# A dynamic 1x1 convolution on one Trainium2 core: the hidden layer's sum over partitions moved off TensorE

## What is computed

```
B, C, H, W = 32, 512, 56, 56;  A = 32 hidden units;  K = 4 kernels
g = group_norm(x, 32 groups)                         # x: (B, 512, 56, 56) float32
pooled = mean(g, over H, W)
h = relu(((pooled @ fc_w.T) - abn_m) * abn_g / sqrt(abn_v + eps) + abn_b)    # first attention layer
ch_att, fl_att = sigmoid(h @ ch_w.T + ch_b), sigmoid(h @ fl_w.T + fl_b)
kn_att = softmax(h @ kn_w.T + kn_b)
agg_w = sum_k kn_att[k] * weight[k]                  # one 512 x 512 matrix for each sample
y = (agg_w @ (g * ch_att)) * fl_att                  # 1x1 convolution
out = x + batch_norm(y)
```

## Time and profile before

| | |
|---|---|
| median of 3 runs | 2103.95 us (2103.34 to 2104.27) |
| span of the profiled execution | 2101.4 us |
| the same, with what lies around the span (the runs' median less the span) | 2.5 us more |
| PE busy | 2054.3 us (98%), 10848 matmuls |
| DVE busy | 1898.9 us (90%) |
| ACT busy | 1726.0 us (82%) |
| POOL busy | 12.8 us (1%) |
| DMA, mean busy share and rate | 58.3% of 16 engines in SyncE's queue, 198 GB/s of HBM traffic |
| mean granted TensorE clock | 0.996 |

### The profile page before, as it was taken

How to read it: one execution, slowest core, us unless ns; L and a number is a source line. 1 busy time by engine, 2 the same in 40 slices (tenths; PEclk the granted TensorE clock), 3 DMA queues, 4 the chain that set the end, 5 groups by cost and what they waited for, 6 DMA issues and landing times.

```text
span 2101.4 us, 33109 instructions
## 1 busy us (share of the span) xinstructions
PE 2054.3 (98%) x10848; PEld 1061.1 (50%) x10848; DVE 1898.9 (90%) x3065; ACT 1726.0 (82%) x2307; POOL 12.8 (1%) x25
## 2 busy tenths in 40 slices
PE   3979999999999999999999999999999999999999
PEld 2535555555555555555555555555555555555554
DVE  8879999999999999999999999999999999999974
ACT  5858888888888888888888888888888888888885
POOL 0100000000000000000000000000000000000000
PEclk9999999999999999999999999999999999999999
DMA  9976656565556565556655566655565655566522
GB/s 334 224 217 207 207 189 206 204 210 199 195 199 206 196 210 196 205 193 209 208 195 203 188 205 207 210 196 194 200 206 199 210 194 204 195 208 207 180 105 106
DMA packets 239644, 421.60 MB, mean 201 GB/s; under 512 B 7552, under 2 KB 236928, under 8 KB 239616
## 3 DMA queue, kind: packets, MB, share of 16 engines
q1 hardware_dynamic: 237888, 415.74, 58.3%
q0 software_dynamic: 1728, 5.51, 1.4%
HBM read 210.19 MB, written 205.52 MB: 198 GB/s over the span
## 4 chain that ended last, share of the span: by engine, by line
PE 93%; DMA 5%; DVE 1%; ACT 1%; SPq 0%; issue 0%; POOL 0%; DVEq 0%; POOLq 0%
PE product L854 31%; PE product L856 31%; PE product L855 31%; DMA out<-x_ring 3%; DMA x_ring<-x 1%; DMA x_ring<-y 1%; PE small L821 0%; SPq L216 0%; DVE chunk_stats L441 0%; ACT w_hi L344 0%; ACT x_norm L262 0%; DVE mixed_weight L625 0%; ACT x_hi L328 0%; DVE x_ring L455 0%; ACT x_hi L271 0%
## 5 line engine op out<-in xcount | busy, mean ns | idle before, releaser
L854 PE MATMUL product<-x_hi,w_hi 128*128 128x448 f16 x3552 | 1253.2, 353 | 11.7 <-DVE x_lo L449 10.3
L855 PE MATMUL product<-x_lo,w_hi 128*128 128x448 f16 x3552 | 1253.1, 353 | 0.0
L856 PE MATMUL product<-x_hi,w_lo 128*128 128x448 f16 x3552 | 1253.0, 353 | 0.0
L283 ACT ACTIVATE y<-product,out_bias,out_scale 128x448 f32<-128x448 f32 x892 | 638.7, 716 | 262.3 <-PE product L856 259.0
L262 ACT ACTIVATE x_norm<-x_ring,norm_bias,norm_scale 128x448 f32<-128x448 f32 x892 | 668.2, 750 | 0.0
L455 DVE TENSOR_TENSOR x_ring<-x_ring,y 128x896 f32<-128x896 f32 x434 | 465.4, 1084 | 80.3 <-ACT y L283 76.0
L854 PEld LDWEIGHTS product<-x_hi,w_hi 128*128 128x128 f16 x3552 | 350.3, 99 | 337.8 <-DVE x_lo L449 11.2
L441 DVE BATCH_NORM_STATS2 chunk_stats<-x_ring 128x6 f32<-128x448 f32 x896 | 492.2, 612 | 22.6 <-DMA x_ring<-x 20.4
L856 PEld LDWEIGHTS product<-x_hi,w_lo 128*128 128x128 f16 x3552 | 347.8, 98 | 324.1 <-issue 1.3
L855 PEld LDWEIGHTS product<-x_lo,w_hi 128*128 128x128 f16 x3552 | 347.8, 98 | 321.1 <-issue 2.9
L449 DVE TENSOR_TENSOR x_lo<-x_norm,x_hi 128x1792 f16<-128x1792 f32 x222 | 447.6, 2016 | 14.9 <-ACT x_hi L271 14.9
(11 more groups left out here) (93 smaller groups left out, 327.8 us busy)
## 6 DMA issues: line engine op xcount, KB each, us to landing
x_ring<-x SPq DMA_DIRECT2D x224, 896.0 KB, 4.8
out<-x_ring SPq DMA_DIRECT2D x223, 896.0 KB, 3.9
x_ring<-y POOLq DMA_DIRECT2D x12, 448.0 KB, 7.5
weight<-wt SPq DMA_DIRECT2D x8, 512.0 KB, 12.9
out<-x_ring SPq DMA_DIRECT2D x4, 224.0 KB, 1.9
params<-par SPq DMA_DIRECT2D x1, 462.0 KB, 12.1
```

The costliest lines, as they stand in the source:

```text
L283: nc.scalar.activation(y[:, s % 2, t], acc[k % BANKS][:, 0:COLS], ACT.Identity, bias=obias[:, t:t + 1], scale=oscale[:, u, t:t + 1]).then_ ...
L854: nc.tensor.matmul(bank, whi[:, u, t, cols], hi, start=(t == 0), stop=False)
L855: nc.tensor.matmul(bank, whi[:, u, t, cols], lo, start=False, stop=False)
L856: ins = nc.tensor.matmul(bank, wlo[:, u, t, cols], hi, start=False, stop=(t == CT - 1))
```

## The change

From the third sample on, the first layer's sum over partitions is made in another way. VectorE turns `fc_sums` in blocks of 32 x 32 (`fcs_t`), so that partition 32q + a holds hidden unit a's 32 terms of quarter q, and sums them to one number for each partition (`fcq`). SyncE writes these 128 numbers to HBM (`rows`), waits until they have landed, and reads them back, all 128 into each partition (`hidq`). VectorE sums the four quarters. For this SyncE has a new step between the load at n = 2 and the store of chunk n = 3, and the steps from `logits` on have later places in `usual`. The first two samples keep the matmul.

More of the change, by code:

```diff
@@ L140, in build @@
         hid_p = small[:, 256:256 + HIDDEN]
+        rows = nc.dram_tensor("hidden_rows", (P,), f32).ap()
         top_row, top_all = small[0:1, 64:64 + P], small[:, 200:201]
@@ L170, in build @@
         pooled_ready = sem("pooled_ready")
+        rows_order = sem("rows_order")
+        hid_summed = sem("hid_summed")
+        fcq_ready = sem("fcq_ready")
+        rows_out = sem("rows_out")
+        rows_in = sem("rows_in")
         logits_ready = sem("logits_ready")
@@ L512, in group_var, with norms @@
                 step(nc.vector.tensor_copy(gm[:, :], grouped[:, 0, 0:CT, 0]))
-            def norms(turn, b):
+            def norms(turn, b, on_pe):
                 u = b % 2
@@ L526, in norms, with logits @@
                 after(turn)
-                nc.vector.tensor_reduce(fcs[:, :], fcp[:, :, :].rearrange("p t a -> p a t"), AX.X,
-                                        ALU.add).then_inc(pooled_ready, 1)
-            def logits(turn, b):
-                dve.wait_ge(hid_done, turn.at(2, b + 1))
-                step(nc.vector.tensor_tensor(hid[:, :], hid_p, p_("abn_m"), ALU.subtract))
+                ins = nc.vector.tensor_reduce(fcs[:, :], fcp[:, :, :].rearrange("p t a -> p a t"), AX.X, ALU.add)
+                if on_pe:
+                    ins.then_inc(pooled_ready, 1)
+                    return
+                ins.then_inc(rows_order, 1)
+                dve.wait_ge(rows_order, turn.at(4, 2 * b - 3))
+                nc.vector.transpose(fcs_t[:, :], fcs[:, :]).then_inc(rows_order, 1)
+                dve.wait_ge(rows_order, turn.at(4, 2 * b - 2))
+                nc.vector.reduce_sum(fcq[:, :], fcs_t[:, :], AX.X).then_inc(fcq_ready, 1)
+            def logits(turn, b, on_pe):
+                if on_pe:
+                    dve.wait_ge(hid_done, b + 1)
+                    step(nc.vector.tensor_tensor(hid[:, :], hid_p, p_("abn_m"), ALU.subtract))
+                else:
+                    dve.wait_ge(rows_in, turn.at(32, 16 * (b - 1)))
[3 more added lines that the diff above has]
+                    step(nc.vector.tensor_tensor(hid[:, :], hid[:, :], p_("abn_m"), ALU.subtract))
                 after(turn)
@@ L609, in _ @@
             group_var(start, 0)
-            norms(start, 0)
+            norms(start, 0, True)
             dve.wait_ge(bn_ready, 1)
-            logits(start, 0)
+            logits(start, 0, True)
             attentions(start, 0)
@@ L731, in body @@
                         if prepare and (n, t) == at["norms"]:
-                            norms(turn, b)
+                            norms(turn, b, at is early)
                         if prepare and (n, t) == at["att"]:
@@ L749, in body @@
                             if (n, t) == at["logits"]:
-                                logits(turn, b)
+                                logits(turn, b, at is early)
                             if (n, t) in at["mix"]:
@@ L817, in _, with hidden @@
         def _(pe):
-            def hidden(turn, b):
-                pe.wait_ge(pooled_ready, turn.at(2, b + 1))
+            def hidden(b):
+                pe.wait_ge(pooled_ready, b + 1)
                 nc.tensor.matmul(hid_p, ones[:, :], fcs[:, :], start=True, stop=True).then_inc(hid_done, 1)
@@ L825, in _ @@
             pe.wait_ge(const_ready, 1)
-            hidden(start, 0)
+            hidden(0)
             def keep_awake(n):
```

4 lines of the change are left out of this document (added).

## The result

The changed kernel takes 2314.77 us (median of 4 runs, 2314.19 to 2318.12), against 2103.66 for the kernel before on the same chip: a ratio of 1.101 (95% interval 1.0997 to 1.1024), 211 us slower. Predicted were 2147 us and a range up to 2172. The sign was right, the size was not: the forecast of +43 was a fifth of what happened, and the prediction is wrong.

A forecast was written before the change was run, and what follows sets the result against it. TensorE was taken to bound the kernel. Per sample -0.25 + 0.18 + 1.51 = +1.44 us, times 30 = +43.2, gave 2147 us, with the transfers costing nothing; the range given was 2136 to 2172.

The forecast's parts named there:

- What goes: On TensorE, the matmul of ones leaves 30 samples, saving 0.25 us each, 7.5 us in all.
- VectorE ahead of chunk 4: VectorE's turning and sum delay chunk 4's x_lo by 0.46 us, making TensorE wait 0.18 us per sample.
- The new places: Chain from ScalarE's mix to chunk 7's x_lo ends later; TensorE waits 1.51 us in each of 30 samples.
- the term of the loss: TensorE's wait for x_lo of chunk 7, each sample's first chunk: 1.51 us, the largest term of +1.44 per sample.
- The two transfers: SyncE's write and read behind the load: rows there at 991.8, in time for VectorE, costing nothing.
- its upper end of 996.6: Latest landing of the read, taking full chunks' landings of 3.9 and 4.8 us behind the load.
- The text's second estimate: Rows' arrival at 992.0 instead of 991.8, from a cited fixed cost of about 2.0 us per transfer; still in time.
- The one-for-one rule: Each microsecond the rows land past 992.2 delays attentions, mix and all behind by one; one late microsecond gives 2177.
- Rival 2: Rows land late at VectorE: up to 4.4 us a sample, +132, a time of 2279; chance 0.10.
- 992.2: Latest time the transfers may land without delaying VectorE's logits and the attentions, on the profiled sample's clock.
- the room of 0.2: Attentions are there at 996.5, 0.2 us before ScalarE's mix can start, so the rows have that slack.
- Rival 4: TensorE's clock falls at each new wait: 3.2 us each, +95 more, a time of 2242; chance 0.02.

The follow-up runs named there:

- experiment 1: Kernel before with only the later places of the changed one, matmul of ones kept, no transfers: 2151.73 us against 2102.21.
- experiment 2: Changed kernel with both transfers left out, the quarter sums VectorE adds being a constant: 2150.05 us, ratio 1.0226.
- experiment 4: Changed kernel with each of the 128 numbers written to, and each partition reading, a 512-byte HBM line of its own: 2149.81 us.
- experiment 5: Changed kernel with VectorE turning the sums once more, so they leave as 4 rows of 128 bytes: 2158.05 us against 2102.95.
- experiment 7: Changed kernel writing the 128 numbers into one SBUF partition and reading an HBM row never rewritten: 2152.04 us (one run).
- experiment 11: Changed kernel with 34 idle matmuls ahead of chunk 6's first product in the 14 middle turns: 2351.71 us, ratio 1.1194.
- experiment 3: Changed kernel with the write issued ahead of the load of chunk n = 2 instead of behind it: 2311.33 us, ratio 1.0998.
- experiment 9: Changed kernel writing only the first 64 of the 128 four-byte pieces, the rest a constant: 2300.95 us (one run).
- experiment 12: Changed kernel with four 128-byte rows, w_hi and w_lo at (6, 0) and (6, 1), turnings behind chunk 4's x_lo: 2132.95 us against 2102.02.

## Why the prediction was wrong

**What goes: right.** 30 matmuls of 0.25 us. Experiments 1 and 2 show the exchange: with the matmul a sample loses 1.60 us, without it 1.60 + 0.22 - 0.25, and the two times differ by 1.7 us, less than their spread.

**VectorE ahead of chunk 4: right.** Laid out were 0.18 us, measured 0.22. The turning and the sum stand at 0.41 and 0.66 behind `fc_sums`' start (1010.38, 1010.79, 1011.04), as laid out.

**The new places: right.** 1.51 laid out, 1.60 measured, in experiments 1, 2 and 4. The step that I had named as the term of the loss is there, when the rows are in time.

**The two transfers: the step that failed.** "I take the shortest landing twice, but behind the load in the same queue: 987.9 + 1.9 + 0.1 + 1.9 = 991.8." The rows came 12.9 us after the quarter sums ended (1011.23 to 1024.13), in the text's own clock at 997.0 instead of 991.8, and 0.4 past its upper end of 996.6. Neither half was 1.9. The write took 9.0, at least 5 of them for the 128 neighbouring pieces (experiments 4, 5, 7; 7.5 in the last sample, where no load hides a part), and even the upper end of the range, which gave it 3.9 behind the load, was too low (landing 7.7 us after the issue at 984.1): I had borrowed the price of large transfers, whose pieces are 1792 bytes and lie apart, for one of the other kind, although the text itself says that pieces of 4 bytes are nowhere in the trace. The read took 4.2, within the 1.9 to 4.8 of the bounds. In one respect the value taken was too dear: a small write behind the load lands with it, 3.9 us after its own issue, and not 1.9 after the load. The text's second estimate of the same moment, 992.0 from a fixed cost that it cites, failed with the first; the 1.9 us that it called in agreement is the landing of a 224 KB store and says nothing of 4-byte pieces.

**The one-for-one rule: right, and it gives most of the size.** Rival 2 said that past 992.2 every microsecond of lateness costs one in each sample. VectorE's wait is 5.4 us, 5.2 of them past the room of 0.2; 5.2 x 30 = 156, added to the forecast of 2147 this is 2303; measured was 2315. Against experiment 2, which has the same instructions and no transfers, 165 us were lost for 162 of VectorE's waiting. The rival with a chance of 0.10 was what happened, and its price of 2279 at the upper end still fell short.

**The clock: it fell, at waits longer than those I had judged.** Rival 4 asked whether 1.5 us waits bring it down. They don't (0.996 in experiments 1, 2 and 4). Of the changed kernel's 34 waits of 2.7 us and more 30 do, with 59 us of slow matmuls in sum. Experiment 11 shows that those in chunk 6, 53 us, lie beside the late chain and are no term of the sum. Those behind first chunks, 7 us, may be a term: in the changed kernel and in experiments 3, 9 and 11 the loss against experiment 2 exceeds VectorE's wait by 2, 2, 14 and 35 us, and the slow matmuls behind first chunks are 7, 3, 15 and 25.

**What stays open:** the unit within which HBM writes hold each other up, and why they do; why a read behind them is slower by 1.3 us than of a line that is left alone; the later rows and the stalls of experiment 11.

**The mistake in method** was to take the price of an operation that no row shows from large transfers' rows. The range was then drawn 0.8 us past the deadline, where the bounds of the text itself reached 4.4 us past it, and all of that got a chance of 0.10.

## What to carry to other kernels

A handover through memory has to be judged by where its pieces lie, not by its bytes: here 512 bytes took 9.0 us as 128 neighbouring pieces and about as long as the load in front of them, 3.5 to 3.9 us, as soon as they lay 16 bytes or more apart or left as four rows. With an empty queue it was 8.9 us against 1.4 to 2.5. Moving 0.25 us of work off the engine that bounds a kernel pays only if nothing that feeds it comes later: lay the feeding chain out from the bounding engine's own clock to its next need, instruction by instruction, which here gave 1.51 us where 1.60 was measured. And when an added wait sits in the program of an engine with many duties, its lateness is paid by everything queued behind it, here 5.5 us a sample for 5.4 us of waiting.

## What the runs showed of the hardware

- 128 writes of 4 bytes into 512 neighbouring bytes of HBM: 9.0 us to landing behind a load, 7.9 with nothing in front; 64 of them 8.0; 16, 64 or 512 bytes apart 3.9; into one partition of SBUF 4.0. All but the 7.9 stand behind a load. With nothing in front, in one write each: 8.9 neighbouring, 7.4 for 64 of them, 2.5 at 16 bytes, 1.4 at 64 and 512 bytes, 1.9 into SBUF, 1.56 as four rows of 128 bytes.
- In each of these last writes of 128 pieces to HBM the last 4-byte packet is done 1.03 to 1.04 us after the issue, whether it lands at 1.4 or at 8.9.
- A read of one 512-byte line by 128 partitions lands in 2.9 us, of a line for each partition in 1.7, of the line just written in 128 pieces in 4.2 to 4.4 (5.2 behind a load).
- TensorE's granted clock stayed full through waits of 1.6 us, 30 times over. It fell to the lower of its two levels, in which a matmul of 448 columns starts every 0.37 us instead of 0.19: in 26 of 30 cases in the first matmuls after waits of 3.2 to 6.8 us, and in all four after waits of 2.68 us; it also fell after the one wait of 2.3 us in experiment 5 and of 2.2 in experiment 12. Eight to sixteen matmuls were slow each time. In experiment 11 it fell after 15 of 29 waits of 2.65 to 2.8 us.
